# Attention with row maxima in four groups per image, formed 19 steps later in the loop, with 52 tiles in front of it instead of 128

## The chip, the cores and the metric

The kernel runs on one core of one Trainium2 chip. The metric is the time of one execution on the device in microseconds. The median of three runs before the change is 5044.32 us (5043.72 to 5045.41).

The core has five engines with a queue each: TensorE (PE; its weight loads are PEld), VectorE (DVE), ScalarE (ACT), GpSimd (POOL) and SyncE (SP, which here only issues DMAs).

## The reference, cut to what matters

The model is a chain of layers over 16 images of 32 x 32 pixels and 128 channels: a binary convolution, a linear attention, the attention that the change touches, a mixture of experts, a grouped attention and a routed layer. The part in question is this, with 16 images (`b`), 1024 tokens each (`n`), 8 search heads of 16 channels and 2 retrieval heads:

```
sq = (x @ wq_s).reshape(b, n, S, DH).transpose(0, 2, 1, 3) * scale
sk = (x @ wk_s).reshape(b, n, S, DH).transpose(0, 2, 1, 3)
rv = (x @ wv_r).reshape(b, n, R, DH).transpose(0, 2, 1, 3)
search_sim = jnp.einsum('bsid,bsjd->bsij', sq, sk)
search_attn = jax.nn.softmax(search_sim, axis=-1)
retrieved = jnp.einsum('bsij,brjd->bsird', search_attn, rv)
...
retrieval_attn = jax.nn.softmax(retrieval_sim, axis=-1)
out = jnp.einsum('bsir,bsird->bsid', retrieval_attn, retrieved)
return out @ w_out
```

## The kernel before, in words

`phase_attn` (L1311) works through the 16 images one after the other. For each image it forms the 1024 x 1024 scores of 8 heads transposed, keys on the partitions and queries along the columns, as 128 tiles of 128 x 512 (**scores**, L1573, into `at_S`). ScalarE takes the exponential of each (L1712, into `at_P`). TensorE multiplies them by the values (**values**, L1584, into `at_num`), GpSimd adds two steps' tiles (L1471, `at_pairs`), and TensorE sums the pairs over the keys (**totals**, L1595, into `at_den`, in even steps).

An image is 32 **steps** of four scores, four exponentials and one values (eight instructions of the profile). Steps 0 to 7 are group 0, 8 to 15 group 1 and so on: group g is half g // 2 of the queries and heads 4 to 7 or 0 to 3 (quad g % 2). The scores are formed two steps ahead: those of step 8 within step 6, those of step 0 of the next image within step 30. TensorE runs in order; a step is scores with side work between them, then values.

The softmax needs the largest score of each query. Since scores stand transposed, a second set of matmuls forms them the other way round (queries on the partitions) as 128 **maxima tiles** (L1541, into `at_side`), and VectorE reduces each to a column (L1638). When all tiles of a group are reduced, VectorE takes the maximum over the two key halves, negated (L1642, `at_negmax`), TensorE transposes this to rows (**rows**, L1546), and VectorE splits the rows into three bf16 terms (L1653 to L1659: the **row chain**, four instructions, each waiting for the one before it). SP copies these three terms with three DMAs into three extra contraction rows of the queries `at_qo` (L1417), where three constant rows of ones in `at_ko` face them, so that the score matmul subtracts the maximum. Group and row work together are a **row group** here.

Before the change a row group covers four heads and all queries. The maxima of image b + 1 are formed within image b, four tiles a step, as **side work** between the scores. Side work shares three banks (`at_side`), taken in turn: a side matmul waits until VectorE has drained the one three before it. The rest of the side work is four transposes of sums per step in steps 3 to 6 and 19 to 22 (`tokens`, L1553), and `back` and `wout` in steps 5, 6, 22 and 23. Which step holds what is set by constants (L1268 to L1280) and by `side_work`; PE and DVE walk through the same list. The maxima of image 0 have no image before them, so 128 tiles and two row groups stand in front of the loop.

SP issues all loads in one queue. The operands of an image come in two halves (z, four heads each) of 12 DMAs of 128 KB; `rows` in SP waits for VectorE's row chain. `over` peels images 0, 1, 14 and 15 and runs 2 to 13 as a hardware loop whose body is two images.

Of the kernel before, what the change touches and what calls it, by code (L numbers as in the profile page):

```python
# [1310 lines left out]
def phase_attn(nc, K, D, X):  # L1311

    SIDE0 = MAX_UNITS + 2
    SIDE1 = sum(len(side_work(k, True, False)) for k in range(STEPS))
# [3 lines left out]
    with Mem(nc, "at") as m:  # L1318
        qo = [m.sb(f"qo{u}", [KM, SH, N], BF16) for u in range(2)]
        ko = [m.sb(f"ko{u}", [KM, SH, N], BF16) for u in range(2)]  # L1320
# [23 lines left out]
        op_in = [[m.sem(f"op_in{u}{z}") for z in range(2)] for u in range(2)]  # L1344
        row_in = [[m.sem(f"row_in{u}{z}") for z in range(2)] for u in range(2)]
        u_in = [m.sem("u_in0"), m.sem("u_in1")]
# [46 lines left out]
        def loads(b, u):  # L1393

            return 96 * (b - u) + 192

        def rows_count(b, u):
            return 24 * (b - u) + 48

        with nc.Block() as block:  # L1400
            @block.sync
            def _(sp):
                sp.dma_start(wout[:, :], D["w_out"]).then_inc(w_in, 16)

                def load(b, u, z):

                    for side_of, (dst, terms) in enumerate(((qo[u], Q_TERMS), (ko[u], K_TERMS))):
                        for i, t in enumerate(terms):
                            sp.dma_start(dst[DH * i:DH * i + DH, QUAD * z:QUAD * z + QUAD, :],
                                         D["qk"][side_of, t, 64 * z:64 * z + 64, bass.ds(b * N, N)]  # L1410
                                         .rearrange("(s d) n -> d s n", d=DH)).then_inc(op_in[u][z], 16)

                def rows(b, u, z):

                    sp.wait_ge(row_ready, 2 * b + z + 1)
                    for t in range(3):
                        sp.dma_start(qo[u][KQ + t:KQ + t + 1, QUAD * z:QUAD * z + QUAD, :], mrow[z][:, t, :])\  # L1417
                          .then_inc(row_in[u][z], 16)

# [9 lines left out]
                for z in range(2):  # L1429
                    load(1, 1, z)  # L1430
                for z in range(2):
                    rows(0, 0, z)
# [97 lines left out]
            def _(pe):  # L1530
                pe.wait_ge(w_in, 16)
                pe.wait_ge(const_ready, 2)

                def fill(w, b, u, free, bank):
# [3 lines left out]
                    if kind == "max":  # L1538
                        s, rest = divmod(w[1], 16)
                        i, h = divmod(rest, 2)  # L1540
                        return pe.matmul(side[bank][:, :], qo[1 - u][0:KQ, s, i * C:(i + 1) * C],  # L1541
                                         ko[1 - u][0:KQ, s, h * CH:(h + 1) * CH], start=True, stop=True)
                    if kind == "rows":
                        z = w[1]
                        pe.wait_ge(row_step, 4 * (2 * (b + 1 - z) + z) + 1)
                        return pe.matmul(side[bank][0:32, 0:C], negmax[:, 32 * z:32 * z + 32], K["ident"][:, :], start=True, stop=True)  # L1546
                    if kind == "tokens":
# [17 lines left out]
                def score(b, u, k, i):  # L1565
# [7 lines left out]
                    pe.matmul(S[n % RING][:, :], ko[u][:, h, j * C:(j + 1) * C], qo[u][:, h, half * CH:(half + 1) * CH],  # L1573
                              start=True, stop=True).then_inc(s_ready, 1)
# [23 lines left out]

                for z in range(2):
                    pe.wait_ge(op_in[0][z], 192)  # L1600
                    for n in range(64 * z, 64 * z + 64):
                        fill(("max", n), -1, 1, n + z + 1 - SIDES, (n + z) % SIDES).then_inc(side_ready, 1)
                    fill(("rows", z), z - 1, 1, 65 + 65 * z - SIDES, (64 + 65 * z) % SIDES).then_inc(side_ready, 1)

                def slot(b, u, last):
# [5 lines left out]
                    for k in range(STEPS):  # L1611
                        if not last and k % 16 == 0:
                            pe.wait_ge(op_in[1 - u][k // 16], loads(b + 1, 1 - u))
                        work = side_work(k, first, last)
# [17 lines left out]
            def _(v):  # L1632
                def drain(w, b, u, at, bank):
                    kind = w[0]
                    v.wait_ge(side_ready, at + 1)
                    if kind == "max":
                        n = w[1]
                        v.reduce_max(mx[:, n // 2, n % 2:n % 2 + 1], side[bank][:, :], AX.X).then_inc(side_saved, 1)  # L1638
                        if n % 64 == 63:
                            z = n // 64  # L1640
                            v.wait_ge(side_saved, at + 1)
                            v.tensor_reduce(negmax[:, 32 * z:32 * z + 32], mx[:, 32 * z:32 * z + 32, :], AX.X, ALU.max, negate=True)\  # L1642
                             .then_inc(row_step, 1)
                    elif kind == "rows":
                        z = w[1]
                        of, of_u = (b + 1, 1 - u) if z == 0 else (b, u)
                        base = 4 * (2 * of + z)
                        src = side[bank][0:32, 0:C]
                        if not isinstance(of, int) or of > 0:

                            v.wait_ge(row_in[1 - of_u][z], rows_count(of - 1, 1 - of_u))
                        left = side[bank][0:32, C:2 * C]
                        v.tensor_copy(mrow[z][:, 0, :], src).then_inc(row_step, 1)  # L1653
                        v.wait_ge(row_step, base + 2)
                        v.tensor_tensor(left, src, mrow[z][:, 0, :], ALU.subtract).then_inc(row_step, 1)
                        v.wait_ge(row_step, base + 3)
                        v.tensor_copy(mrow[z][:, 1, :], left).then_inc(row_step, 1)
                        v.wait_ge(row_step, base + 4)
                        v.tensor_tensor(mrow[z][:, 2, :], left, mrow[z][:, 1, :], ALU.subtract).then_inc(row_ready, 1)  # L1659
                        v.wait_ge(row_ready, 2 * of + z + 1)  # L1660
                        v.sem_inc(side_saved, 1)
# [15 lines left out]

                for z in range(2):
                    for n in range(64 * z, 64 * z + 64):
                        drain(("max", n), -1, 1, n + z, (n + z) % SIDES)  # L1680
                    drain(("rows", z), z - 1, 1 - z, 64 + 65 * z, (64 + 65 * z) % SIDES)

# [1051 lines left out]
```

## Time and profile before

| | us |
|---|---|
| profiled execution, whole time | 5044.79 |
| its span, first to last instruction | 5043.0 |
| median of 3 runs | 5044.32 |
| attention: first maxima tile | 1280.17 |
| attention: first score | 1360.84 |
| maxima reductions (L1638), busy on VectorE, 2048 of them | 1294.2 |
| exponentials (L1712), busy on ScalarE, 2048 of them | 1120.4 |
| pair additions (L1471), busy on GpSimd, 256 of them | 1159.9 |
| granted TensorE clock, mean (1.0 is 2.4 GHz, 0.5 is 1.2 GHz) | 0.905 |

An instruction row of the timeline gives its start in us from the span's start, its duration (several alike are merged, with their count), the engine, the line of the kernel, what it writes and reads, and in brackets how long the engine was idle before it and what ended that. Matmuls overlap, so the distance between starts tells more than their durations.

### The profile page before, as it was taken

To read this page: it belongs to the slowest core of one execution; us is meant where nothing else is said; L and a number is where in the kernel's file an instruction comes from. 1 tells how busy PE (TensorE), PEld (TensorE's weight loads), DVE (VectorE), ACT (ScalarE), POOL (GpSimd) and SP (SyncE) were. 2 spreads that over 40 slices of the span, in tenths; PEclk is the share of its full clock that TensorE was granted. 3 is DMA by queue.
4 is the path that set the end of the run, shared out by engine and by line. 5 is a ranking of instruction groups with operands and counts; after the bars stand their busy time and mean duration, and the time that the engine had idled before them with its cause. 6 is when DMAs were issued, how large, how long until landed. Compare 5 with 4: busy or idle time off the path is not lost. (4 is left out here: it accounts for less than half of the span.)

```text
span 5043.0 us, 74851 instructions
## 1 busy us (share of the span) xinstructions
PE 4215.2 (84%) x23003; PEld 1647.9 (33%) x23003; DVE 2938.1 (58%) x5302; ACT 2179.4 (43%) x4008; POOL 1824.4 (36%) x1333
## 2 busy tenths in 40 slices
PE   5399999937899999999999999966999999855513
PEld 2143434325122222222222222223444444443312
DVE  4778878747777767676767677534000000357774
ACT  3332323237166656565656566653343343511400
POOL 1100000027267767676767677871000000210401
PEclk9699999969599999999999999987999999956655
DMA  1265555437422222222222222011000000110504
GB/s 72 50 134 116 120 118 118 99 139 275 62 32 32 32 32 32 32 32 32 32 32 32 32 32 32 8 48 39 0 0 0 0 0 0 59 67 37 200 0 146
DMA packets 178141, 296.64 MB, mean 59 GB/s; under 512 B 43511, under 2 KB 102909, under 8 KB 175373
## 3 DMA queue, kind: packets, MB, share of 16 engines
q1 hardware_dynamic: 149640, 257.12, 22.6%
q10 hardware_dynamic: 23808, 25.17, 1.4%
q0 software_dynamic: 4368, 10.07, 0.7%
q8 instruction: 197, 3.23, 0.3%
q14 instruction: 128, 1.05, 0.1%
HBM read 94.49 MB, written 69.73 MB: 33 GB/s over the span
## 5 line engine op out<-in xcount | busy, mean ns | idle before, releaser
L1638 DVE TENSOR_REDUCE at_mx<-at_side 128x1 f32<-128x512 f32 x2048 | 1294.2, 682 | 417.0 <-PE at_side L1541 406.0
L1712 ACT ACTIVATE at_P<-at_S 128x512 f32<-128x512 f32 x2048 | 1120.4, 600 | 751.6 <-PE at_S L1573 701.9
L1471 POOL TENSOR_TENSOR at_pairs<-at_P 128x2048 f32<-128x2048 f32 x256 | 1159.9, 4531 | 318.2 <-ACT at_P L1712 297.5
L1573 PE MATMUL at_S<-at_qo,at_ko 99*128 99x512 bf16 x2048 | 786.4, 389 | 75.4 <-ACT at_P L1712 74.4
L1541 PE MATMUL at_side<-at_ko,at_qo 96*128 96x512 bf16 x2048 | 789.9, 399 | 44.2 <-DMA at_ko<-qk 23.3
L1989 ACT ACTIVATE ff_hs<-ff_ph,ff_b 128x512 f32<-128x512 f32 x512 | 351.7, 687 | 524.5 <-PE ff_ph L1959 524.5
L1584 PE MATMUL at_num<-at_P,at_rvt 128*32 128x512 f32 x4096 | 552.2, 612 | 0.0
L1959 PE MATMUL ff_ph<-ffn_Y,ff_w 128*128 (+1 forms) x1024 | 525.0, 595 | 8.6 <-DMA ff_b<-in_b_dram 8.6
L1973 PE MATMUL ff_po<-ff_hs,ff_w2s 128*128 128x512 f32 x1024 | 522.8, 592 | 0.0
L2008 DVE SCALAR_TENSOR_TENSOR X<-ff_po,ffn_b2w,X 128x512 f32 (+1 forms) x32 | 24.0, 751 | 823.0 <-PE ff_po L1973 823.0
L819 DVE SCALAR_TENSOR_TENSOR la_dwq<-la_pad,la_taps,la_dwq 128x1024 f32<-128x1024 f32 x384 | 491.5, 1280 | 11.6
L1573 PEld LDWEIGHTS at_S<-at_qo,at_ko 99*128 99x128 bf16 x2048 | 196.9, 98 | 886.6 <-ACT at_P L1712 679.2
L1068 POOL TENSOR_TENSOR n_ln_ab<-n_ln_mv,eps 128x4 f32<-128x4 f32 x96 | 19.1, 199 | 1207.4 <-DVE n_ln_mv L1059 1205.7
L634 PE MATMUL la_acc<-la_rep,la_wagg 128*32 128x512 f32 x2560 | 318.1, 616 | 3.9 <-DMA la_rep<-la_pad 3.1
L596 POOL DMA_DIRECT2D proj<-la_y x32 | 17.4, 544 | 812.5 <-ACT la_y L905 812.5
L1541 PEld LDWEIGHTS at_side<-at_ko,at_qo 96*128 96x128 bf16 x2048 | 201.6, 99 | 325.5 <-DVE at_mx L1638 136.3
L1595 PE MATMUL at_den<-at_pairs,ones 128*32 128x512 f32 x2048 | 277.9, 615 | 5.9 <-POOL at_pairs L1471 5.9
L1959 PEld LDWEIGHTS ff_ph<-ffn_Y,ff_w 128*128 128x128 f32 x1024 | 195.6, 191 | 254.0 <-issue 244.7
L1973 PEld LDWEIGHTS ff_po<-ff_hs,ff_w2s 128*128 128x128 f32 x1024 | 194.7, 190 | 245.1 <-issue 244.6
L1083 ACT ACTIVATE n_ln_xt<-n_ln_front,n_ln_ab 128x128 f32<-128x128 f32 x384 | 144.3, 456 | 107.2 <-POOL n_ln_ab L1074 91.9
L613 PE MATMUL la_acc<-X,la_wqkv 128*128 (+1 forms) x192 | 88.2, 611 | 90.6 <-POOLq L592 82.9
L1584 PEld LDWEIGHTS at_num<-at_P,at_rvt 128*32 128x32 f32 x4096 | 81.4, 108 | 190.8 <-issue 109.4
(410 smaller groups left out, 4538.0 us busy)
## 6 DMA issues: line engine op xcount, KB each, us to landing
la_rep<-la_pad SPq DMA_DIRECT2D x512, 162.8 KB, 3.6
qk<-ap_part SPq DMA_DIRECT2D x32, 768.0 KB, 3.7
at_qo<-qk SPq DMA_DIRECT2D x192, 128.0 KB, 4.7
at_ko<-qk SPq DMA_DIRECT2D x192, 128.0 KB, 7.8
n_ln_xs<-X SPq DMA_DIRECT2D x96, 256.0 KB, 2.3
u<-ap_us SPq DMA_DIRECT2D x32, 320.0 KB, 4.0
X<-in_x_dram SPq DMA_DIRECT2D x4, 2048.0 KB, 25.5
proj<-la_y POOLq DMA_DIRECT2D x32, 256.0 KB, 5.0
```

The costliest lines, as they stand in the source:

```text
L634: done = pe.matmul(acc[c][32 * j:32 * j + 32, :], wagg[:, p - 1, j, g, :], view(slice(0, C), p, h, j, *PLACES[g]), start=(c < 2 and g == 0 ...
L819: v.scalar_tensor_tensor(out, image, taps[:, t:t + 1], out, ALU.mult, ALU.add).then_inc(tap_done, 1)
L1471: g.tensor_tensor(pairs[i % 2][:, :, :], P[a][:, :, :], P[a + 1][:, :, :], ALU.add).then_inc(pair_done, 1)
L1541: return pe.matmul(side[bank][:, :], qo[1 - u][0:KQ, s, i * C:(i + 1) * C], ko[1 - u][0:KQ, s, h * CH:(h + 1) * CH], start=True, stop=True)
L1573: pe.matmul(S[n % RING][:, :], ko[u][:, h, j * C:(j + 1) * C], qo[u][:, h, half * CH:(half + 1) * CH], start=True, stop=True).then_inc(s_r ...
L1584: last = pe.matmul(num[32 * i:32 * i + 32, :], rvt[u][:, j, :], P[k % SLOTS][:, i, :], start=(j == 0), stop=(j == 7))
L1595: last = pe.matmul(den[32 * i:32 * i + 32, :], K["ones"][:, 0:32], pairs[(k // 2 - 1) % 2][:, i, :], start=(j == 0), stop=(j == 6))
L1638: v.reduce_max(mx[:, n // 2, n % 2:n % 2 + 1], side[bank][:, :], AX.X).then_inc(side_saved, 1)
L1712: a.activation(P[k % SLOTS][:, i, :], S[(4 * k + i) % RING][:, :], ACT.Exp).then_inc(p_ready, 1)
L1959: pe.matmul(ph[j % R][:, :], w1[:, f, :], Y[:, bass.ds(b * N + half * CH, CH)], start=True, stop=True).then_inc(h_mm, 1)
L1973: done = pe.matmul(po[half][:, :], w2s[u][:, f, :], hs[j % R][:, :], start=(f == 0), stop=(f == FT - 1)).then_inc(h_used, 1)
L1989: a.activation(hs[j % R][:, :], ph[j % R][:, :], ACT.Gelu, bias=b1[:, j % FT:j % FT + 1]).then_inc(h_ready, 1)
```

## The change

The maxima of an image are formed in four row groups instead of two, each half of the queries and four heads: group j is exactly what the scores of steps 8j to 8j + 7 need. They are formed 19 steps later: tiles 0 to 51 of image b + 1 in steps 19 to 31 of image b, tiles 52 to 127 in steps 0 to 18 of image b + 1 itself. Only 52 tiles and one row group stand in front of the loop, and the last image has maxima in its steps 0 to 18. The rows of groups 0, 1, 2 and 3 are made in steps 27, 3, 11 and 19, at the end of the step's side work and no longer at its start. The queries are laid out by half, so their loads are 12 DMAs of 64 KB in place of 6 of 128 KB for each half of the heads. SP loads both halves of image b + 1 at the end of image b - 1 where it loaded one of them there and the other (of the image after) eight steps before. The wait for the constant rows moves behind the tiles in front of the loop.

```diff
-ROWS_AT = (17, 1)
+MAX_AT = 19
+ROWS_AT = (27, 3, 11, 19)
+GROUP = 32
+LOADS = 16 * (2 * len(Q_TERMS) + len(K_TERMS))
...
     if post:
-        if k == ROWS_AT[1]:
-            work.append(("rows", 1))
...
-    if not last:
-        if k == ROWS_AT[0]:
-            work.append(("rows", 0))
-        work += [("max", n) for n in range(QUAD * k, QUAD * k + QUAD)]
+    ahead = k >= MAX_AT
+    if not ahead or not last:
+        n = QUAD * ((k - MAX_AT) % STEPS)
+        work += [("max", n + i, int(ahead)) for i in range(QUAD)]
+    for j in range(4):
+        if k == ROWS_AT[j] and (j or not last):
+            work.append(("rows", j))
     return work
 
+LEAD = QUAD * (STEPS - MAX_AT)
+
+def tile_of(n):
+
+    j, rest = divmod(n, GROUP)
+    half, quad = divmod(j, 2)
+    s, rest = divmod(rest, 8)
+    i, h = divmod(rest, 2)
+    return QUAD * quad + s, QUAD * half + i, h
...
-        qo = [m.sb(f"qo{u}", [KM, SH, N], BF16) for u in range(2)]
+        qo = [m.sb(f"qo{u}", [KM, 2, SH, CH], BF16) for u in range(2)]
...
-        mrow = [m.sb(f"mrow{z}", [32, 3, C], BF16) for z in range(2)]
+        mrow = [m.sb(f"mrow{j}", [16, 3, C], BF16) for j in range(4)]
...
                         sp.wait_ge(s_ready, HEADS * b)
-                        load(b + 1, 1 - u, 1)
+                        for z in range(2):
+                            load(b + 1, 1 - u, z)
                     if not last:
                         wait_if(sp, pv_done, 32 * b)
                         values_of(b + 1, 1 - u)
                     if not is_first(b):
-                        rows(b, u, 1)
                         if not isinstance(b, int) or b > 1:
 
                             sp.wait_ge(side_ready, side_at(b - 1, ("back", 1)))
                         search_of(b - 1, 1)
-                        sp.wait_ge(side_ready, side_at(b, ("back", 0), last))
+                    rows(b, u, 1)
+
+
+                    rows(b, u, 2)
+                    search_of(b, 0)
+                    rows(b, u, 3)
                     if not last:
                         rows(b + 1, 1 - u, 0)
-                    search_of(b, 0)
-                    if not isinstance(b, int) or b < B - 2:
-
-                        sp.wait_ge(s_ready, HEADS * b + 96)
-                        load(b + 2, u, 0)
...
-                    if k in (0, 8) and i == 0:
-                        pe.wait_ge(row_in[u][quad], rows_count(b, u))
+                    if j == 0 and i == 0:
+                        pe.wait_ge(row_in[u][g], rows_count(b, u))
...
-                for z in range(2):
-                    pe.wait_ge(op_in[0][z], 192)
-                    for n in range(64 * z, 64 * z + 64):
-                        fill(("max", n), -1, 1, n + z + 1 - SIDES, (n + z) % SIDES).then_inc(side_ready, 1)
-                    fill(("rows", z), z - 1, 1, 65 + 65 * z - SIDES, (64 + 65 * z) % SIDES).then_inc(side_ready, 1)
+                for n in range(LEAD):
+                    if n % GROUP == 0:
+                        pe.wait_ge(op_in[0][n // GROUP], LOADS)
+                    fill(("max", n, 1), -1, 1, n + 1 - SIDES, n % SIDES).then_inc(side_ready, 1)
+                fill(("rows", 0), -1, 1, LEAD + 1 - SIDES, LEAD % SIDES).then_inc(side_ready, 1)
+                pe.wait_ge(const_ready, 2)
```

In front of the loop the order of TensorE's instructions was this before (L1541 maxima tiles, L1546 rows, L1573 scores).

```order
L1541 MATMUL at_side<-at_ko,at_qo 128x512 x64
L1546 MATMUL at_side<-ident,at_negmax 32x128
L1541 MATMUL at_side<-at_ko,at_qo 128x512 x64
L1546 MATMUL at_side<-ident,at_negmax 32x128
L1573 MATMUL at_S<-at_qo,at_ko 128x512 x9
```

In the changed kernel, whose line numbers are 19 to 20 higher here, the same place reads as follows.

```order
L1560 MATMUL at_side<-at_ko,at_qo 128x512 x52
L1566 MATMUL at_side<-ident,at_negmax 16x128
L1593 MATMUL at_S<-at_qo,at_ko 128x512 x9
L1560 MATMUL at_side<-at_ko,at_qo 128x512
L1593 MATMUL at_S<-at_qo,at_ko 128x512
```

One row group follows the 52 tiles directly, and the scores of image 0, which need its rows, follow that.

Within the loop, this is TensorE's step 17 of image 0 before, from the values of step 16 to those of step 17.

```order
L1584 MATMUL at_num<-at_P,at_rvt 32x512 x4
L1573 MATMUL at_S<-at_qo,at_ko 128x512
L1546 MATMUL at_side<-ident,at_negmax 32x128
L1573 MATMUL at_S<-at_qo,at_ko 128x512
L1541 MATMUL at_side<-at_ko,at_qo 128x512 x2
L1573 MATMUL at_S<-at_qo,at_ko 128x512
L1541 MATMUL at_side<-at_ko,at_qo 128x512
L1573 MATMUL at_S<-at_qo,at_ko 128x512
L1541 MATMUL at_side<-at_ko,at_qo 128x512
L1584 MATMUL at_num<-at_P,at_rvt 32x512 x4
```

And this is step 27 of image 0 in the changed kernel, from values to values (L1604).

```order
L1604 MATMUL at_num<-at_P,at_rvt 32x512 x4
L1593 MATMUL at_S<-at_qo,at_ko 128x512
L1560 MATMUL at_side<-at_ko,at_qo 128x512
L1593 MATMUL at_S<-at_qo,at_ko 128x512
L1560 MATMUL at_side<-at_ko,at_qo 128x512 x2
L1593 MATMUL at_S<-at_qo,at_ko 128x512
L1560 MATMUL at_side<-at_ko,at_qo 128x512
L1593 MATMUL at_S<-at_qo,at_ko 128x512
L1566 MATMUL at_side<-ident,at_negmax 16x128
L1604 MATMUL at_num<-at_P,at_rvt 32x512 x4
```

The rows matmul has moved from the first side place of its step to the last, directly ahead of values.

On SP, image 1 before issues its DMAs in this order (L1409 operand loads, L1421 values, L1417 rows, L1424 search inputs; the last two rows are the load of the image after next).

```order
L1409 DMA at_qo<-qk 16x4x1024 x6
L1409 DMA at_ko<-qk 16x4x1024 x6
L1421 DMA at_rvt<-u 128x8x32
L1417 DMA at_qo<-at_mrow 1x32x128 x3
L1424 DMA at_ub<-u 128x4x128
L1417 DMA at_qo<-at_mrow 1x32x128 x3
L1424 DMA at_ub<-u 128x4x128
L1409 DMA at_qo<-qk 16x4x1024 x6
L1409 DMA at_ko<-qk 16x4x1024 x6
```

In the changed kernel image 1 has this (L1426 and L1430 operand loads, L1439 rows).

```order
L1426 DMA at_qo<-qk 16x4x512 x12
L1430 DMA at_ko<-qk 16x4x1024 x6
L1426 DMA at_qo<-qk 16x4x512 x12
L1430 DMA at_ko<-qk 16x4x1024 x6
L1443 DMA at_rvt<-u 128x8x32
L1446 DMA at_ub<-u 128x4x128
L1439 DMA at_qo<-at_mrow 1x16x128 x6
L1446 DMA at_ub<-u 128x4x128
L1439 DMA at_qo<-at_mrow 1x16x128 x6
```

All 36 loads of the next image now stand together at the front, and the first rows of the image stand behind them and behind both smaller loads.

## Rows read from the trace of the kernel before

**Rows 1.** Costliest groups: busy us, mean ns, then idle before and who ended it.

```profile
L1638 DVE TENSOR_REDUCE at_mx<-at_side 128x1 f32<-128x512 f32 x2048 | 1294.2, 682 | 417.0 <-PE at_side L1541 406.0
```

**Rows 2.** Timeline of PE in front of the loop: start, duration, what, idle before.

```profile
1280.17 37.84 PE L1541 MATMUL at_side<-at_ko,at_qo 96*128 96x512 bf16 x64 [23.34 <-DMA at_ko<-qk]
...
1360.84 4.42 PE L1573 MATMUL at_S<-at_qo,at_ko 99*128 99x512 bf16 x9
```

**Rows 3.** Timeline of DVE in front of the loop.

```profile
1280.79 38.35 DVE L1638 TENSOR_REDUCE at_mx<-at_side 128x1 f32<-128x512 f32 x64 [22.89 <-PE at_side L1541]
```

**Rows 4.** Stretch in front: length, PE, PEld, DVE, ACT, POOL busy, PEclk, DMA share, GB/s.

```profile
1266.00:1313.00 47.00, 32.83 (x56) 5.84 (x56) 32.21 (x54) 0.00 (x0) 13.29 (x2) 0.50 1.06 139
```

**Rows 5.** Line 1417, the row DMAs: ns per issue, and landing.

```profile
L1417 SPq DMA_DIRECT2D at_qo<-at_mrow x96: 502/584/595, 1321.4 to 3246.1; - x96
...
DMA to landing us min/median/max: 1.8/1.9/3.6
```

**Rows 6.** Timeline of PE, values of steps 10 and 11 of image 6.

```profile
2153.09 1.06 PE L1584 MATMUL at_num<-at_P,at_rvt 128*32 128x512 f32 x8
...
2155.94 1.07 PE L1584 MATMUL at_num<-at_P,at_rvt 128*32 128x512 f32 x8
```

**Rows 7.** Timeline of DVE, steps 11, 17 and 19 of image 6.

```profile
2154.74 2.48 DVE L1638 TENSOR_REDUCE at_mx<-at_side 128x1 f32<-128x512 f32 x4 [0.69 <-PE at_side L1541]
...
2176.17 0.28 DVE L1653 CAST at_mrow<-at_side 32x128 bf16<-32x128 f32 x1 [0.90 <-PE at_side L1546]
...
2177.12 0.28 DVE L1659 TENSOR_TENSOR at_mrow<-at_side,at_mrow 32x128 bf16<-32x128 f32 x1
...
2185.07 2.43 DVE L1638 TENSOR_REDUCE at_mx<-at_side 128x1 f32<-128x512 f32 x4
```

**Rows 8.** Timeline of PE, step 17 of image 6, and the values of step 19.

```profile
2174.31 1.07 PE L1584 MATMUL at_num<-at_P,at_rvt 128*32 128x512 f32 x8
...
2175.63 0.41 PE L1546 MATMUL at_side<-ident,at_negmax 128*32 128x128 f32 x2
2175.97 0.39 PE L1573 MATMUL at_S<-at_qo,at_ko 99*128 99x512 bf16 x1
...
2177.51 0.39 PE L1541 MATMUL at_side<-at_ko,at_qo 96*128 96x512 bf16 x1 [0.51 <-DVEq L1661]
...
2178.69 1.07 PE L1584 MATMUL at_num<-at_P,at_rvt 128*32 128x512 f32 x8
...
2186.09 1.07 PE L1584 MATMUL at_num<-at_P,at_rvt 128*32 128x512 f32 x8
```

**Rows 9.** Line 1584 in two stretches of 18 steps: length, PE, PEld, clock, DMA.

```profile
3120.81:3189.70 68.89, 19.18 (x145) 2.84 (x145) 1.00 0.08 13
3241.72:3297.58 55.86, 19.21 (x148) 2.87 (x149) 1.00 0.04 11
```

**Rows 10.** Timeline of SP, the load in front of image 2.

```profile
1595.01 2.74 SPq L1409 DMA_DIRECT2D at_qo<-qk x6
```

**Rows 11.** Two stretches at the first jump back, columns as in rows 4.

```profile
1840.00:1852.00 12.00, 7.04 (x44) 1.79 (x40) 5.54 (x11) 3.39 (x7) 6.96 (x4) 0.89 0.99 133
1852.00:1864.00 12.00, 10.12 (x41) 2.02 (x37) 5.28 (x12) 6.36 (x12) 5.76 (x2) 0.69 0.09 15
```

**Rows 12.** Timeline of PE, the first score of step 6 of image 2.

```profile
1627.68 0.39 PE L1573 MATMUL at_S<-at_qo,at_ko 99*128 99x512 bf16 x1
```

**Rows 13.** Line 995, the loop's branch: ns min/median/max, first and last start.

```profile
L995 ACTq COMPARE_BRANCH  x6: 40/45/50, 1843.4 to 3113.1; - x6
...
L995 PEldq COMPARE_BRANCH  x6: 83/3498/3785, 1851.2 to 3115.8; - x6
...
L995 DVEq COMPARE_BRANCH  x6: 55/63/63, 1852.8 to 3117.4; - x6
...
L995 ACTq FUSED_REGOPS  x5: 59/59/65, 1850.0 to 2865.3; - x5
...
L995 DVEq FUSED_REGOPS  x5: 74/74/74, 1855.6 to 2871.1; - x5
```

More of the change, by code:

```diff
@@ L1344, in phase_attn @@
         op_in = [[m.sem(f"op_in{u}{z}") for z in range(2)] for u in range(2)]
-        row_in = [[m.sem(f"row_in{u}{z}") for z in range(2)] for u in range(2)]
+        row_in = [[m.sem(f"row_in{u}{j}") for j in range(4)] for u in range(2)]
         u_in = [m.sem("u_in0"), m.sem("u_in1")]
@@ L1393, in loads @@
         def loads(b, u):
-            return 96 * (b - u) + 192
+            return LOADS // 2 * (b - u) + LOADS
         def rows_count(b, u):
@@ L1405, in load, with rows @@
                 def load(b, u, z):
[L1407 to L1410, printed above, removed]
-                                         .rearrange("(s d) n -> d s n", d=DH)).then_inc(op_in[u][z], 16)
-                def rows(b, u, z):
-                    sp.wait_ge(row_ready, 2 * b + z + 1)
+                    heads = slice(QUAD * z, QUAD * z + QUAD)
+                    for i, t in enumerate(Q_TERMS):
+                        for half in range(2):
+                            sp.dma_start(qo[u][DH * i:DH * i + DH, half, heads, :],
+                                         D["qk"][0, t, 64 * z:64 * z + 64, bass.ds(b * N + half * CH, CH)]
+                                         .rearrange("(s d) n -> d s n", d=DH)).then_inc(op_in[u][z], 16)
+                    for i, t in enumerate(K_TERMS):
+                        sp.dma_start(ko[u][DH * i:DH * i + DH, heads, :],
+                                     D["qk"][1, t, 64 * z:64 * z + 64, bass.ds(b * N, N)]
+                                     .rearrange("(s d) n -> d s n", d=DH)).then_inc(op_in[u][z], 16)
+                def rows(b, u, j):
+                    half, quad = divmod(j, 2)
+                    sp.wait_ge(row_ready, 4 * b + j + 1)
                     for t in range(3):
-                        sp.dma_start(qo[u][KQ + t:KQ + t + 1, QUAD * z:QUAD * z + QUAD, :], mrow[z][:, t, :])\
-                          .then_inc(row_in[u][z], 16)
+                        sp.dma_start(qo[u][KQ + t:KQ + t + 1, half, QUAD * quad:QUAD * quad + QUAD, :],
+                                     mrow[j][:, t, :]).then_inc(row_in[u][j], 16)
                 def values_of(b, u):
@@ L1430, in _ @@
                     load(1, 1, z)
-                for z in range(2):
-                    rows(0, 0, z)
+                rows(0, 0, 0)
                 def slot(b, u, last):
@@ L1538, in fill @@
                     if kind == "max":
[L1539 to L1542, printed above, removed]
+                        s, i, h = tile_of(w[1])
+                        of_u = 1 - u if w[2] else u
+                        return pe.matmul(side[bank][:, :], qo[of_u][0:KQ, i // QUAD, s, i % QUAD * C:(i % QUAD + 1) * C],
+                                         ko[of_u][0:KQ, s, h * CH:(h + 1) * CH], start=True, stop=True)
                     if kind == "rows":
-                        z = w[1]
-                        pe.wait_ge(row_step, 4 * (2 * (b + 1 - z) + z) + 1)
-                        return pe.matmul(side[bank][0:32, 0:C], negmax[:, 32 * z:32 * z + 32], K["ident"][:, :], start=True, stop=True)
+                        j = w[1]
+                        of = b if j else b + 1
+                        pe.wait_ge(row_step, 4 * (4 * of + j) + 1)
+                        return pe.matmul(side[bank][0:16, 0:C], negmax[:, 16 * j:16 * j + 16], K["ident"][:, :], start=True, stop=True)
                     if kind == "tokens":
@@ L1570, in score @@
                     wait_if(pe, p_ready, HEADS * b + (n - 2 if n >= RING else n - 1 if n < 2 else -2))
-                    if k in (0, 8) and i == 0:
-                        pe.wait_ge(row_in[u][quad], rows_count(b, u))
-                    pe.matmul(S[n % RING][:, :], ko[u][:, h, j * C:(j + 1) * C], qo[u][:, h, half * CH:(half + 1) * CH],
+                    if j == 0 and i == 0:
+                        pe.wait_ge(row_in[u][g], rows_count(b, u))
+                    pe.matmul(S[n % RING][:, :], ko[u][:, h, j * C:(j + 1) * C], qo[u][:, half, h, :],
                               start=True, stop=True).then_inc(s_ready, 1)
@@ L1611, in slot @@
                     for k in range(STEPS):
-                        if not last and k % 16 == 0:
-                            pe.wait_ge(op_in[1 - u][k // 16], loads(b + 1, 1 - u))
+                        if not last and k in (MAX_AT, MAX_AT + 8):
+                            pe.wait_ge(op_in[1 - u][(k - MAX_AT) // 8], loads(b + 1, 1 - u))
                         work = side_work(k, first, last)
@@ L1638, in drain @@
                         v.reduce_max(mx[:, n // 2, n % 2:n % 2 + 1], side[bank][:, :], AX.X).then_inc(side_saved, 1)
[L1639 to L1640 removed]
+                        if n % GROUP == GROUP - 1:
+                            j = n // GROUP
                             v.wait_ge(side_saved, at + 1)
[L1642 removed]
+                            v.tensor_reduce(negmax[:, 16 * j:16 * j + 16], mx[:, 16 * j:16 * j + 16, :], AX.X, ALU.max, negate=True)\
@@ L1643, in drain @@
                              .then_inc(row_step, 1)
                     elif kind == "rows":
[L1645 to L1648, printed above, removed]
+                        j = w[1]
+                        of, of_u = (b, u) if j else (b + 1, 1 - u)
+                        base = 4 * (4 * of + j)
+                        src = side[bank][0:16, 0:C]
@@ L1649, in drain @@
                         if not isinstance(of, int) or of > 0:
-                            v.wait_ge(row_in[1 - of_u][z], rows_count(of - 1, 1 - of_u))
-                        left = side[bank][0:32, C:2 * C]
-                        v.tensor_copy(mrow[z][:, 0, :], src).then_inc(row_step, 1)
+                            v.wait_ge(row_in[1 - of_u][j], rows_count(of - 1, 1 - of_u))
+                        left = side[bank][0:16, C:2 * C]
+                        v.tensor_copy(mrow[j][:, 0, :], src).then_inc(row_step, 1)
@@ L1654, in drain @@
                         v.wait_ge(row_step, base + 2)
-                        v.tensor_tensor(left, src, mrow[z][:, 0, :], ALU.subtract).then_inc(row_step, 1)
+                        v.tensor_tensor(left, src, mrow[j][:, 0, :], ALU.subtract).then_inc(row_step, 1)
                         v.wait_ge(row_step, base + 3)
-                        v.tensor_copy(mrow[z][:, 1, :], left).then_inc(row_step, 1)
+                        v.tensor_copy(mrow[j][:, 1, :], left).then_inc(row_step, 1)
                         v.wait_ge(row_step, base + 4)
-                        v.tensor_tensor(mrow[z][:, 2, :], left, mrow[z][:, 1, :], ALU.subtract).then_inc(row_ready, 1)
@@ L1660, in drain @@
-                        v.wait_ge(row_ready, 2 * of + z + 1)
+                        v.tensor_tensor(mrow[j][:, 2, :], left, mrow[j][:, 1, :], ALU.subtract).then_inc(row_ready, 1)
+                        v.wait_ge(row_ready, 4 * of + j + 1)
                         v.sem_inc(side_saved, 1)
@@ L1676, in invert @@
                     v.reciprocal(sm1[:, :], sm1[:, :]).then_inc(rsum_ready, 1)
[L1678 to L1681, printed above, removed]
+                for n in range(LEAD):
+                    drain(("max", n, 1), -1, 1, n, n % SIDES)
+                drain(("rows", 0), -1, 1, LEAD, LEAD % SIDES)
                 def slot(b, u, last):
```

4 lines of the change are left out of this document (1 added, 3 removed).

## The prediction

> **What bounds the kernel now.** I read three places, each in the timeline: the stretch in front of the attention loop, ordinary steps of the loop, and the last image, which has no maxima.
>
> In front of the loop VectorE sets the pace. It reduces 64 tiles in 38.35 us [rows 3], 0.60 us a tile, at a TensorE clock of 0.50 (1.2 GHz) [rows 4]; TensorE feeds it from 1280.17 us and makes its first score at 1360.84 us [rows 2]: 80.7 us for 128 tiles and two row groups. The loads run beside it; 48 of 128 KB, 6.3 MB, fill the DMA engines until about 1313 us at 139 GB/s [rows 4].
>
> Inside the loop the 682 ns reductions are the largest group, but VectorE sits idle 417 us before them, 406 us of that for TensorE [rows 1]: TensorE is the bound. A step is read from one values matmul (the ones into at_num) to the next. Step 11 of image 6, with no totals and nothing extra, runs from 2153.09 to 2155.94 us: 2.85 us [rows 6]. Its four reductions take 2.48 us and start 0.69 us after the previous ones ended [rows 7]. VectorE has slack on average, yet only three side banks cover it.
>
> The last image shows what maxima cost under scores: 18 steps take 68.89 us in image 14 and 55.86 us in image 15 (144 values matmuls each; the two counts of 145 and 148 include a few at the cuts) [rows 9].
>
> **The change part by part.** The sum is made against the profiled execution, 5044.8 us, half a us above the median of the runs, so the same total holds for both. What a measurement of this kernel can tell from no change is 0.2%, 10 us.
>
> *Front.* 52 tiles of 0.60 us after the first reduction at 1280.79 end at 1312.0 us, 1312.2 with the reduction to 16 columns between them. The start does not move: it waits for the first half of the loads (the engine's releaser is at_ko from DRAM [rows 2]), and that half has the same bytes. The wait for the two constant rows, which moves behind this stretch, is covered by that. Then, for the first time, the front's end is exposed: the row chain on VectorE (2176.17 to 2177.40, 1.2 us [rows 7]), three DMA issues of 0.58 us and a landing of 1.9 us [rows 5]. The first score comes at 1312.2 + 1.3 + 1.2 + 1.9 = 1316.6 us instead of 1360.84: **-44 us**. Those DMAs stand behind all loads in SP's queue, which end at 1313, just in time.
>
> *Row groups.* Four instead of two an image. Cost before: step 17 runs from 2174.31 to 2178.69, 4.38 us where a plain one takes 2.85 [rows 8, 6], so 1.5 us; two make 3.0 an image. Some 0.4 us of it is the matmul's own slot (0.34 from its start to the next score's, and a little ahead of it), the other 1.1 us is waiting for side banks: the group's matmul stands first in the step, the chain of 1.2 us holds up four reductions, and the matmul at 2177.51 waits until the chain has ended (0.51 us idle, releaser DVE) [rows 8]. In the new order the group's matmul is the last one of its step; behind it come values (1.0 us), scores and maxima. Replayed in steps 11 and 27: the last reduction ends 1.3 us after the old start of values [rows 6, 7] and the chain 2.5 us after it, under values and the next step's scores. Its bank is wanted only by the third side matmul after it, which comes behind values (1.0), two side matmuls, three scores and the totals (1.0), over 3.5 us after that same point. So the slot of 0.4 us is left, with some friction 0.5. In steps 3 and 19, which also hold four transposes, VectorE is behind already: in step 19 the reductions from 2185.07 take 2.43 us and end 1.4 us after values started at 2186.09 [rows 7, 8]. With two more side matmuls ahead of values, and the chain behind them, replaying bank by bank gives values 0.7 us later and the totals 0.86 us later; I take 0.86. Four groups: 2 x 0.5 + 2 x 0.86 = 2.7 against 3.0. For 14 images, 1 to 14: **-4 us**. The ends of this price are 0.4 us (matmul alone) and 1.5 us (as now).
>
> *Image 0* had one group in the loop and now has four: 2.7 - 1.5 = **+1.2 us**.
>
> *Image 15* gets maxima in steps 0 to 18. The image 14 stretch (steps 1 to 18) holds two old groups; 68.89 - 3.0 - 55.86 = 10.0, a share of 0.6 for step 0, and new groups at 3 and 11 (1.4): **+12 us**. Groups at 19 fall where ScalarE has the pace and cost nothing.
>
> *Row waits.* Scores of group 1 start at step 6, of 2 at 14, of 3 at 22, of 0 at 30; each group's matmul is at the end of the third step before. Chain, issues and landing take 1.3 + 1.2 + 1.9 = 4.4 us, plus up to 1 us in which VectorE is late; the two steps between are at least 2 x 2.85 us, and values of the step with the group 1.0 more: 6.7 us. Hidden for 2, 3, 0. Group 1 stands behind the load burst. Before, heads 4 to 7 of the next image were loaded once step 29 had made the last score, and heads 0 to 3 of the one after it 8 steps earlier; now both halves, 36 DMAs, go at the end of step 29. In front of image 2 SP starts the twelve that stood there at 1595.01 [rows 10]; a burst of this kind moves 133 GB/s [rows 11]. By bytes 3.15 MB take 24 us, from about 1596, values and search inputs (0.39 MB) 3 more, to 1623; the rows land by 1625. They are needed at 1627.68 [rows 12], less 1.5 (old group in step 1 gone) plus 0.9, so 1627.1. **0**, with 2 us to spare.
>
> The Trainium skill (DMA: Bandwidth & Descriptors, its table of measured HBM to SBUF transfers) says "Transfers under 64 KB are descriptor-dominated" and gives 0.95 us for one of 64 KB. Taken per DMA, that would make the burst about as long as 36 of the present ones. The present 128 KB loads move at about 1.0 us each [rows 4, 11], and no run so far shows one of 64 KB from this source.
>
> *Loop-back.* Images 2 to 13 run as a hardware loop of two images, so five jumps back. On the first of them ScalarE branches at 1843.4 and goes on at 1850.0 (6.6 us), VectorE at 1852.8 and 1855.6 (2.8 us), TensorE's branch takes 3.5 us in the median [rows 13]. The load burst fills the DMA engines to 1852 and not after: share 0.99, then 0.09 [rows 11]. I read that as instruction fetch slowed by the burst: 6.6 us inside, 2.8 to 3.5 outside. With both halves in one burst, to about 1864, TensorE's and VectorE's branches fall inside too: 6.6 - 3.5 = 3.1 us, five times, **+16 us**. Bounds: 0 (ScalarE's fetch is simply slower) and 6.6 a jump.
>
> Sum: -44 - 4 + 1.2 + 12 + 16 = -18.8; 5044.8 - 18.8 = **5026 us**.
>
> **Rivals.**
> 1. *The row groups stay dear* (slower). Reductions that come late hold the banks wherever the chain stands: 1.5 us each. Then 6.0 instead of 2.7 an image, 15 times, and 1.6 more in the last: +51, 5077 us. For it: TensorE waits for VectorE at every group now. Against: values and totals follow the chain in the new order. The sum is level with before when each of the 62 groups in the loop costs 0.3 us more, 0.98 instead of the mean 0.68.
> 2. *The burst costs by DMA, not by byte* (slower). 36 x 1.0 us plus 3 and the landing ends at 1637, 10 us late at step 6; nine image boundaries without a jump pay it, 90 us. In front, 72 loads end at 1266 + 70 = 1336 and the first score 20 us later. 5026 + 110 = 5136 us. For it: each DMA writes only 16 partitions, in shorter runs than before, and that form is in no row. Against: the two bursts shown move 133 and 139 GB/s with rather different work beside them [rows 4, 11], which looks like a limit on bytes. Decides from a burst of 26 us on.
> 3. *The jumps do not grow.* 5026 - 16 = 5010 us. For it: different engines are compared.
> 4. *Half-way*: groups near 0.98 us, or somewhat less and a few short waits at step 6. 5044 us.
>
> **How the numbers follow.** Forecast 0.50 (5015 to 5037, 0.05 of it inside 10 us of before), rival 3 0.15, rival 4 0.14, rival 1 0.12, rival 2 0.09. Faster 0.45 + 0.15 = 0.60; same 0.05 + 0.14 = 0.19; slower 0.21. The range runs from 5005 (rival 3 with groups at 0.5) to 5080 (rival 1); it leaves out rival 2 and about as much again in tails.
>
> **What would show it.** First score near 1317 us, with 52 reductions at 0.60 ahead. Steps 1 and 17 at 2.85 us; 11 and 27 at 3.3; 3 and 19 longer by 0.7. No wait of a score for a DMA at step 6, and a burst of 24 us. TensorE's branch at about 6.6 us. The first 18 steps of image 15 at 67 to 68 us. Wrong if the side matmuls after a group still idle for VectorE over 0.5 us, if the burst goes past 26 us, or if ScalarE's own branch lengthens.

## The result, and the profile after

The changed kernel takes 4979.32 us in the median of four runs (4974.1 to 4982.09); the kernel before takes 5044.86 in the runs beside it. The ratio is 0.9871, 95% interval 0.9858 to 0.9884: 65 us faster. Forecast were 5026 us and a range of 5005 to 5080. The direction was right, the size was wrong by more than three times, and the time lies outside the range.

The profiled execution has a span of 4980.2 us instead of 5043.0, 62.8 less. In front of the loop TensorE's timeline now reads (start, duration, what, idle before):

```profile
1278.48 20.51 PE L1560 MATMUL at_side<-at_ko,at_qo 96*128 96x512 bf16 x35 [23.92 <-DMA at_ko<-qk]
1299.20 10.18 PE L1560 MATMUL at_side<-at_ko,at_qo 96*128 96x512 bf16 x17 [0.21 <-DVE at_mx L1659]
1309.36 0.61 PE L1566 MATMUL at_side<-ident,at_negmax 128*16 128x128 f32 x2
1314.78 4.33 PE L1593 MATMUL at_S<-at_qo,at_ko 99*128 99x512 bf16 x9 [4.81 <-DMA at_qo<-at_mrow]
```

This answers to [rows 2]. There are 52 tiles, the start is still set by the operand loads, and the wait of 4.81 us for the row DMAs is new. The attention's first DMA is issued at 1263.24 us, where it was 1265.52 before (the code ahead of it is the same; over the ten kernels profiled here this issue lies between 1261.2 and 1266.1 us). From that issue to the first score it is 51.5 us, before 95.3: 43.8 us less.

An ordinary step with a row group, step 11 of image 6, in the timelines of TensorE and VectorE:

```profile
2098.42 1.06 PE L1604 MATMUL at_num<-at_P,at_rvt 128*32 128x512 f32 x8
...
2101.49 0.28 PE L1566 MATMUL at_side<-ident,at_negmax 128*16 128x128 f32 x1
2101.51 0.63 PE L1604 MATMUL at_num<-at_P,at_rvt 128*32 128x512 f32 x3
...
2105.62 1.07 PE L1604 MATMUL at_num<-at_P,at_rvt 128*32 128x512 f32 x8
```

```profile
2100.06 2.49 DVE L1659 TENSOR_REDUCE at_mx<-at_side 128x1 f32<-128x512 f32 x4 [0.46 <-PE at_side L1560]
2102.46 0.27 DVE L1674 CAST at_mrow<-at_side 16x128 bf16<-16x128 f32 x1
...
2103.40 0.28 DVE L1680 TENSOR_TENSOR at_mrow<-at_side,at_mrow 16x128 bf16<-16x128 f32 x1
```

The step is 3.09 us long (2098.42 to 2101.51) and the next 4.11, where plain ones are 2.85 and 3.95: the group costs 0.40 us. The reader sees why in the second fence: the chain of four runs from 2102.46 to 2103.68, while TensorE is in values and in the next step's scores. In [rows 8] the same chain stood in TensorE's way. Over the whole run TensorE's side matmuls sat idle until the chain's end 30 times before, 13.4 us in all, and never in the changed kernel. A group in step 3 costs 0.59 us (3.84 and 4.57 where 3.45 and 4.38 stood).

The loop's branch, ns min/median/max and first and last start, answers to [rows 13]:

```profile
L995 ACTq COMPARE_BRANCH  x6: 40/45/50, 1794.6 to 3042.0; - x6
L995 PEldq COMPARE_BRANCH  x6: 76/4968/5592, 1798.5 to 3044.6; - x6
...
L995 ACTq FUSED_REGOPS  x5: 59/59/65, 1797.4 to 2796.1; - x5
```

TensorE's branch has grown from 3.5 to 5.0 us (medians). ScalarE, which took 6.6 us from its branch (1843.4) to the next instruction (1850.0), now takes 2.8 (1794.6 to 1797.4).

Image lengths, from one image's first values matmul to the next's in the timeline, give the whole account. "Jump" are the images 3, 5, 7, 9 and 11, at whose end the hardware loop jumps back; "ordinary" are the other nine of 1 to 14. For these two the first columns are the length of one image, and change and forecast are those of all of them together.

| part | before | after | change | forecast |
|---|---|---|---|---|
| front, first DMA to first score | 95.3 | 51.5 | -43.8 | -44 |
| image 0 | 116.8 | 117.2 | +0.4 | +1.2 |
| 9 ordinary images, mean | 122.16 | 121.17 | -8.9 | -2.6 |
| 5 images with a jump, mean | 131.46 | 128.09 | -16.8 | +14.6 |
| image 15 | 96.6 | 107.4 | +10.8 | +12 |
| the rest: ahead of the attention and behind its last values | | | -4.5 | 0 |

### The profile page after: what moved, and what is told of

Read it like the earlier page. It is cut to its first block and busy times, and to the rows that moved or that the text cites. A ratio compares the mean times of both kernels' runs of the same rounds, so it can differ in the third digit from the quotient of the medians.

```text
span 4980.2 us, 75881 instructions
## 1 busy us (share of the span) xinstructions
PE 4171.5 (84%) x23066; PEld 1649.2 (33%) x23067; DVE 2975.5 (60%) x5462; ACT 2175.7 (44%) x4008; POOL 1825.0 (37%) x1333
## 5 line engine op out<-in xcount | busy, mean ns | idle before, releaser
L1560 PE MATMUL at_side<-at_ko,at_qo 96*128 96x512 bf16 x2048 | 777.5, 390 | 29.1 <-DMA at_ko<-qk 23.9
L1604 PE MATMUL at_num<-at_P,at_rvt 128*32 128x512 f32 x4096 | 557.5, 606 | 0.0
L1604 PEld LDWEIGHTS at_num<-at_P,at_rvt 128*32 128x32 f32 x4096 | 91.3, 108 | 175.7 <-issue 103.5
```

The source lines that it names most:

```text
L1560: return pe.matmul(side[bank][:, :], qo[of_u][0:KQ, i // QUAD, s, i % QUAD * C:(i % QUAD + 1) * C], ko[of_u][0:KQ, s, h * CH:(h + 1) * CH] ...
L1604: last = pe.matmul(num[32 * i:32 * i + 32, :], rvt[u][:, j, :], P[k % SLOTS][:, i, :], start=(j == 0), stop=(j == 7))
```

## The experiments

### The place of the row group

**Rows first.** The changed kernel with the rows matmul back at the head of its step:

```diff
+    for j in range(4):
+        if k == ROWS_AT[j] and (j or not last):
+            work.append(("rows", j))
     if not ahead or not last:
         n = QUAD * ((k - MAX_AT) % STEPS)
         work += [("max", n + i, int(ahead)) for i in range(QUAD)]
-    for j in range(4):
-        if k == ROWS_AT[j] and (j or not last):
-            work.append(("rows", j))
```

> The changed kernel, but the rows matmul stands ahead of the four maxima matmuls of its step, as in the kernel before, instead of behind them. Theory P (place): a row group then costs 1.3 to 1.5 us again instead of 0.4 to 0.6, some 62 groups, 45 to 60 us more: 5025 to 5040 us. Theory Q (a group of 16 rows is cheaper than one of 32 wherever it stands): the time stays within 10 us of 4979.

5038.02 us, ratio 0.9991 (0.9981 to 1.0). TensorE's timeline, step 3 of an image:

```profile
2122.98 0.39 PE L1566 MATMUL at_side<-ident,at_negmax 128*16 128x128 f32 x2
2124.75 0.39 PE L1560 MATMUL at_side<-at_ko,at_qo 96*128 96x512 bf16 x1 [0.41 <-DVEq L1682]
```

The wait for VectorE at the end of the chain (L1682) is back; over the whole run it comes 62 times, 30.9 us in all. Step 11 takes 4.27 us and step 3 4.91, so a group costs 1.4 to 1.5 us, and an ordinary image takes 124.95 us. Theory P holds and Q falls: 16 rows are no cheaper than 32. The chain's four instructions last as long as before, 1.2 us. The place alone is worth 59 us here, more than the 44 us of the shorter front.

**Rows last, before.** The kernel before with its two groups moved behind the maxima of their step:

```diff
-    if post:
-        if k == ROWS_AT[1]:
-            work.append(("rows", 1))
...
-        if k == ROWS_AT[0]:
-            work.append(("rows", 0))
         work += [("max", n) for n in range(QUAD * k, QUAD * k + QUAD)]
+        if k == ROWS_AT[0]:
+            work.append(("rows", 0))
+    if post and k == ROWS_AT[1]:
+        work.append(("rows", 1))
```

> The kernel before (two row groups an image, formed ahead in full), but the rows matmul stands behind the four maxima matmuls of its step instead of ahead of them. Theory P (place sets the price of a group: 1.5 us in front, 0.4 us behind): ordinary images shorten from 122.2 to about 120.0 us, 14 images by 30 us, and the kernel takes 5010 to 5018 us. That would be shorter images than the changed kernel's 121.2, since there are two groups and not four. Theory Q (small groups are cheap): no change, 5044 us.

5011.76 us, ratio 0.9935 (0.9917 to 0.9952). Ordinary images take 119.93 us. As theory P says: two groups behind cost less than four behind (121.17) and much less than two in front (122.16).

### The jumps of the hardware loop

**Keys first.** The changed kernel, each half of a load issuing its key DMAs ahead of its query DMAs:

```diff
+                    for i, t in enumerate(K_TERMS):
+                        sp.dma_start(ko[u][DH * i:DH * i + DH, heads, :],
...
                     for i, t in enumerate(Q_TERMS):
                         for half in range(2):
...
-                    for i, t in enumerate(K_TERMS):
-                        sp.dma_start(ko[u][DH * i:DH * i + DH, heads, :],
```

> The changed kernel, but each half of the operand load issues its 6 key DMAs (128 KB, 2 KB runs) ahead of its 12 query DMAs (64 KB, 1 KB runs). In the changed kernel ScalarE's branch at the end of the two-image loop body takes 2.7 to 2.9 us, where it took 6.6 to 7.2 before. Theory A (an instruction fetch queues behind the load bytes that SP has already issued and that have not moved yet; SP issues one DMA in about 0.47 us, a 128 KB one needs 1.0 us, a 64 KB one 0.5): ScalarE's branch, about 4 us after the burst starts, comes behind six 128 KB loads again and takes 5 to 7 us, and the kernel is 10 to 25 us slower than the changed one (4990 to 5005 us). Theory B (the branch got shorter because the program is laid out differently): the branch stays at 2.8 us and the time at about 4979 us.

4988.14 us, ratio 0.9891 (0.9875 to 0.9908). ScalarE's branch:

```profile
L995 ACTq COMPARE_BRANCH  x6: 40/45/50, 1793.1 to 3050.8; - x6
...
L995 ACTq FUSED_REGOPS  x5: 59/59/65, 1798.1 to 2804.9; - x5
```

5.0 us instead of 2.8 at the first jump, and images with a jump 130.09 instead of 128.09 us. The bytes and the number of DMAs are the same; only what has been issued by the time of the branch is different. That speaks for A and against B. The branch (4.6 to 4.9 us) and the time lie just under what A expected; the five jumps give 10 us. The intervals of this ratio and of the changed kernel's overlap a little, so the reading rests on the branch and on the length of these images.

**Query loads split, before.** The kernel before with its query DMAs cut in two:

```diff
+                    for i, t in enumerate(Q_TERMS):
+                        for half in range(2):
+                            sp.dma_start(qo[u][DH * i:DH * i + DH, QUAD * z:QUAD * z + QUAD, half * CH:half * CH + CH],
+                                         D["qk"][0, t, 64 * z:64 * z + 64, bass.ds(b * N + half * CH, CH)]
```

> The kernel before, but each of its 6 query DMAs of 128 KB is issued as two of 64 KB (1 KB runs), everything else as it was. Theory A: ScalarE's branch falls from 6.6 to 7.2 us to about 2.8, TensorE's stays near 3.5 or rises a little, and the five jumps give back 2 to 4 us each: 5025 to 5035 us. Theory B (program layout): no change, 5044 us. Theory C (the burst costs by DMA and not by byte): bursts of 18 us instead of 12.

5036.41 us, ratio 0.9986 (0.9977 to 0.9996). A miss by size: the gain is smaller than A expected. The branches:

```profile
L995 ACTq COMPARE_BRANCH  x6: 40/45/50, 1839.7 to 3103.3; - x6
L995 PEldq COMPARE_BRANCH  x6: 83/5846/5955, 1844.2 to 3105.9; - x6
...
L995 ACTq FUSED_REGOPS  x5: 59/59/65, 1843.0 to 2854.0; - x5
```

ScalarE's branch falls to 3.3 us as expected. But TensorE's, which I expected near 3.5 or a little above, rises to 5.8: ScalarE no longer delays it until the burst is over, so its own fetch meets the burst. Images with a jump exceed ordinary ones by 8.3 us instead of 9.3. Theory C, which expected 18 us, falls: by their first and last packet the bursts last 12.1 to 13.3 us with 18 DMAs, where they last 11.4 to 12.8 with 12.

**Loads late.** The changed kernel with the 36 loads behind the rows of step 3, and the kernel before with its twelve behind the rows of step 1:

```diff
-                    if not last and not is_first(b):
-
-                        sp.wait_ge(s_ready, HEADS * b)
-                        for z in range(2):
-                            load(b + 1, 1 - u, z)
...
                     rows(b, u, 1)
+                    if not last and not is_first(b):
+
+                        sp.wait_ge(s_ready, HEADS * b)
+                        for z in range(2):
+                            load(b + 1, 1 - u, z)
```

> The changed kernel, but SP issues the 36 loads of the next image behind the rows of group 1 (step 3) instead of at the end of the image before, so that no load runs at the loop's jumps back. Theory A: TensorE's branch falls from 5.0 us to 3.5 us or less, VectorE's from 4 to 5 us to 2.8, the jump costs 2 to 4 us less, five times: 4960 to 4972 us. Theory B (burst and jump have nothing to do with each other): 4979 us. A rival that makes it slower: rows of group 2 or 3 come late behind the burst, or maxima at step 19 wait for loads; not expected, the burst of 25 us from step 4 ends near step 11.

4971.11 us, ratio 0.9861 (0.9845 to 0.9878). The intervals of this ratio and of the changed kernel's overlap, so the gain over it rests on the traces: images with a jump 126.17 us instead of 128.09, ordinary ones unchanged at 121.15. ScalarE's branch takes 2.4 to 2.7 us, VectorE's 2.8 to 3.0, and TensorE's is this:

```profile
L995 PEldq COMPARE_BRANCH  x6: 83/3856/4035, 1797.2 to 3033.5; - x6
```

That is above the 3.5 us or less that A expected, and a jump gives back 1.9 us, just under its 2 to 4.

The same on the kernel before:

```diff
-                        load(b + 1, 1 - u, 1)
...
                         rows(b, u, 1)
+                        if not last:
+                            sp.wait_ge(s_ready, HEADS * b)
+                            load(b + 1, 1 - u, 1)
```

> The kernel before, but the twelve loads that SP issued at the end of the image before (heads 4 to 7) are issued behind the rows of step 1, so that no load runs at the five jumps back. Theory A (fetch behind the load backlog): ScalarE's branch falls from 6.9 us to about 2.5, the images with a jump from 131.5 to about 127 us: 5018 to 5028 us. Theory B (program layout of the kernel before): the branch stays at 6.9 us, 5044 us.

5019.64 us, ratio 0.9949 (0.9931 to 0.9967), 25 us faster than before. Images with a jump take 126.74 us instead of 131.46, ScalarE's branch 2.4 to 2.7 instead of 6.6 to 7.2. The DMAs, their sizes and the other engines' instructions are the same; B falls.

### Sum and improvement

**Both, before.** The kernel before with rows last and loads late, by the two edits shown above:

> The kernel before with both edits, rows behind the maxima of their step and the twelve loads behind the rows of step 1; the 128 tiles in front of the loop stay. If the two causes are separate, they add: 4988 to 4998 us. What the changed kernel has beyond it is the shorter front, less the maxima in the last image and the two more groups.

4993.62 us, ratio 0.99 (0.9883 to 0.9918). The two gains, 33 and 25 us, add up to 51 of 58. More than three quarters of the changed kernel's 65 us can thus be had without its four groups and its shorter front.

**Rows early in the front.** The changed kernel with loads late and, in front, the rows after 36 tiles, their DMAs ahead of the loads of image 1:

```diff
+                    if at == LEAD_ROWS:
+                        fill(("rows", 0), -1, 1, at + 1 - SIDES, at % SIDES).then_inc(side_ready, 1)
+                        continue
...
                 values_of(0, 0)
+                rows(0, 0, 0)
                 for z in range(2):
                     load(1, 1, z)
-                rows(0, 0, 0)
```

> The changed kernel with the 36 loads behind the rows of step 3, and in front of the loop the row group 0 formed after 36 of the 52 tiles, its three DMAs issued ahead of the loads of image 1. TensorE waits 4.8 us at the end of the front for these DMAs now; they should land under the last 16 tiles (9.6 us). First score 4 to 5 us earlier, no wait for a DMA ahead of it: 4964 to 4970 us. Rival: the loads of image 1, now issued from 1301 us on, hold up the rows of group 1 at step 3, and the front gives the gain back: 4971 us or more.

4965.97 us, ratio 0.9843 (0.9825 to 0.9861). TensorE's timeline:

```profile
1302.55 0.61 PE L1565 MATMUL at_side<-ident,at_negmax 128*16 128x128 f32 x2
...
1313.30 4.38 PE L1592 MATMUL at_S<-at_qo,at_ko 99*128 99x512 bf16 x9
```

The first score follows the tiles with no wait for a DMA, 47.5 us after the attention's first DMA instead of 51.5. The rival did not occur: image 0, whose group 1 it was about, takes 115.8 us instead of 117.2, with the rows landing 1.3 us ahead of their first score. The median is the lowest of all kernels here, but its interval overlaps that of the changed kernel with loads late (0.9845 to 0.9878), so the last 5 us rest on the front of the trace.

## Why the prediction was right in direction and wrong in size

- **Front, -44: right.** 43.8 us, with the same start rule, 0.60 us a tile, and a new wait of 4.81 us; from the last reduction (1310.50) to the first score it is 4.3 us, which the sum had as 4.4 for chain, issues and landing.
- **Row groups: mechanism right, price too high.** Replayed were 0.5 us (steps 11, 27) and 0.86 (3, 19); measured are 0.40 and 0.59, together 2.0 us an image instead of 2.7, against 3.0 before. That is -1.0 us an image instead of -0.3, 14 us over 14 images instead of 4. No side matmul idled for the chain, so the sign of being wrong that the prediction named (over 0.5 us) did not come. Why steps 3 and 19 lose less than the bank-by-bank replay gave was not followed further. Rival 1 (groups stay dear) has the right price for the wrong place: it is what the kernel with rows first shows, 5038 us, where the shorter front is eaten up.
- **Row waits, 0: right, but with luck.** By its first and last packet a burst lasts 24.4 to 26.5 us where 24 were forecast; four of the 14 pass the 26 us that the prediction named as its limit. The longest is the one in front of image 2, for which it reckoned 2 us to spare: there the rows of group 1 land 0.2 us ahead of the first score of step 6, and 0.2 us in image 14 too; in the other images of 1 to 15 it is 1.9 to 4.2 us. Summed over the whole run, score matmuls and their weight loads wait 5.7 us for row DMAs. 4.8 of these are in front; the other 0.8 is a weight load at that step 6 of image 2, whose matmul starts no later for it (view of the score line 1593: who ended its idle time, us and times):

```profile
  DMA at_qo<-at_mrow: 5.7, 2
```

- **Rival 2 fell.** In a burst 64 KB loads cost about half of 128 KB ones. The Trainium skill's 0.95 us for one of 64 KB (DMA: Bandwidth & Descriptors, its table of measured transfers) is no price for these in a row: 24 of them and 12 of 128 KB move in 24.4 to 26.5 us, 3.15 MB at 119 to 129 GB/s.
- **Image 15, +12: right** (10.8, and 0.7 more in step 0, which counts to image 14).
- **Loop-back, +16: wrong, and the sign with it.** It is the step that failed. The jumps cost 9.3 us each before, 6.9 after: -12 us in all, a difference of 28 us to the forecast, the largest part of the error of 44. The observation behind it (a branch is slow inside a burst) was right, and TensorE's and VectorE's branches did grow, 3.5 to 5.0 and 2.8 to about 4.4 us. But I took "inside a burst" as one state with one price, 6.6 us, and did not ask how much was queued at that moment, so ScalarE's own branch stood in the sum as unchanged and fell to 2.8. ScalarE branches 2.9 us after the first packet. By then SP has begun nine DMAs of 128 KB in the kernel before, and six or seven of 64 KB in the changed one. The change made the first ones 64 KB, a thing it did for the layout of the queries.

| kernel | first DMAs of the burst | ScalarE's branch, us | 8 KB packet begins, us after that branch | TensorE goes on, us after it (mean) | jump minus ordinary, us |
|---|---|---|---|---|---|
| before | 6 x 128 KB, then 128 KB | 6.6 to 7.2 | 4.1 to 4.6 | 11.7 | 9.3 |
| keys first | 6 x 128 KB, then 64 KB | 4.6 to 4.9 | 2.2 to 2.4 | 11.3 | 8.9 |
| before, split | 12 x 64 KB | 3.1 to 3.3 | 0.9 | 10.3 | 8.3 |
| changed | 12 x 64 KB | 2.7 to 2.9 | 0.9 to 1.0 | 9.0 | 6.9 |
| before, loads late | no burst | 2.4 to 2.7 | 0.9 to 1.1 | 7.1 | 4.6 |
| changed, loads late | no burst | 2.4 to 2.7 | 0.9 to 1.2 | 7.6 | 5.0 |

The column on the 8 KB packet shows the wait itself. Between ScalarE's branch and its next instruction each of these kernels has exactly one packet of an instruction queue, q14, of 8 KB. The profile does not say whose it is, but none other begins in that stretch. Below are rows of the view of DMA queues (packets, MB, share of 16 engines) over stretches that begin at the first branch: in the kernel before, 4.0 us (1843.39 to 1847.39) hold loads alone, and 4.3 us (to 1847.69) have the packet too; with loads late (changed kernel) 1.4 us (1793.35 to 1794.75) have it and nothing else.

```profile
q1 hardware_dynamic: 324, 0.53, 109.4%
...
q14 instruction: 1, 0.01, 1.3%
...
q14 instruction: 1, 0.01, 1.4%
```

## What to carry to other kernels

A short dependent chain on one engine is cheap or dear by what the other engine has queued behind it: moved from the head to the end of the side work of its step, the same four instructions cost 0.4 us instead of 1.5. Where an in-order engine jumps back in a hardware loop, keep large loads away from that point, or at least issue small ones first. And when a term rests on a measured slow case, ask what was in the queue in that case, not only whether a queue was there.

## What the runs showed of the hardware that was not expected

- A branch back in this hardware loop, whose body lasts some 250 us, costs ScalarE 2.4 to 2.7 us, VectorE 2.8 to 3.1 and TensorE 3.3 to 4.0 with no load running; GpSimd goes on after 0.25 us in every kernel. In a loop of the same program whose body lasts 20 us, ScalarE goes on after 0.3 us (1137.45 to 1137.74 in the kernel before).
- With a load burst beside it ScalarE's took up to 7.2 us and TensorE's up to 6.0 us. The one instruction packet behind ScalarE's branch began 4.1 to 4.6 us after it with 0.6 to 0.7 MB of loads issued and not moved, and 0.9 to 1.2 us after it with none.
- After such a pause TensorE's clock goes down to its lower level, 1.2 GHz, for a while: at the first jump of the changed kernel it idled 4.1 us behind the values of 1798.74, and the granted clock is 1.00 in the stretch that ends there and 0.72 in the mean of the next (stretch, length, PE, PEld, DVE, ACT and POOL busy, clock, DMA share, GB/s), so the pause costs more than its own length. In the 25 us from ScalarE's branch at the first jump the mean clock is 0.80 before and 0.86 in the changed kernel.

```profile
1791.70:1803.70 12.00, 7.07 (x44) 1.77 (x40) 5.74 (x10) 4.83 (x9) 9.14 (x5) 1.00 0.68 132
1803.70:1815.70 12.00, 11.77 (x52) 2.67 (x52) 6.54 (x10) 6.05 (x11) 5.80 (x3) 0.72 0.91 138
```
